# Composed weights stored once in float32 and split after the load, with the end of the count stage reordered

## The chip, the cores and the metric

The kernel runs on one core of a Trainium2 chip. The metric is device time in microseconds (us), the median of several executions. The engines are TensorE (PE, with its weight loads as PEld), VectorE (DVE), ScalarE (ACT), GpSimd (POOL) and SyncE (SP), which here only issues transfers. Two queues of transfers matter: the one that SyncE fills (q1) and the one that GpSimd fills (q0). All of them are served by the same 16 DMA engines.

## The reference

There are 625 nodes with 512 features and 10000 edges, each with 128 attributes and a type, 0 or 1.

```python
m = relu(concat([h[src], edge_attr]) @ W1.T + b1) @ W2.T + b2
agg = segment_sum(m, dst)
# gates r, z, n of a GRU cell from agg and h, batch norm, residual sum
x = layernorm(x + h + bn)
# then two relational layers (relu between them), each:
w = einsum('rb,bio->rio', att, basis)      # 30 bases of 512x512, 2 relations
msg = where(edge_type == 0, sigmoid(x_j @ gate_w[0]) * x_j @ w[0],
                            sigmoid(x_j @ gate_w[1]) * x_j @ w[1])
out = segment_sum(msg, row) + x @ root + bias
```

and at the end `layernorm(x + out)`. The 30 bases of each layer are 31 MB, so reading `basis` for both layers is most of the traffic.

## The kernel before, in words

Most matrix products are done with each operand split into a high part, rounded to the matmul's input format (fp32r), and a low part, the difference; three products of such parts make one full one. ScalarE writes the high part (a copy with a cast) and VectorE the low part (a subtraction).

The program has these stages.

1. **Count** (to 68 us). For 20 windows of 32 nodes VectorE makes one-hot rows (lines 869 and 874), TensorE counts with them (line 1228), ScalarE copies the counts out (lines 635 and 637). In between TensorE composes the first three weight tiles (line 1203), and multiplies x by a part of W1. After window 19 VectorE works out which windows each unit of edges touches (lines 917 to 928, ten small operations on one partition, the result is `wins`), adds the first three attribute rows (line 939), and drains the third early tile (`drain_early`, line 880). Only then, at line 1316, does TensorE clear its banks and start the units: it waits for `ct_drained` of the last window, `early_drained` of all three early tiles, and `wins_ready`.
2. **Units** (68 to 194 us). 20 units of four groups of 128 edges. GpSimd gathers rows, TensorE multiplies attributes (line 1238) and sums messages (lines 1284, 1285), VectorE adds and splits, ScalarE applies relu (line 667).
3. **Jobs** (194 to 512 us). A list, `plan_jobs`, fixes the order of 86 jobs; all engines walk it. Each job fills one of eight PSUM banks, and the job eight places later reuses the bank. A letter in the list says who drains it, "A" for ScalarE and "V" for VectorE. Kinds are RT, agg, r, hn, in, z (the GRU cell), xT (transposes), w (a composed tile), M (a tile of x times a composed weight) and out.

A composed weight does not come out of TensorE in the layout in which M needs it. So each of 16 tiles (`w`, 8 in each layer, 3 of them early) goes to device memory and comes back. Drain of a tile: ScalarE casts the bank into `ev[:, 0]` (line 729, for early tiles line 658), VectorE subtracts it from the bank into `ev[:, 1]` (line 1080, for early tiles line 880), and SyncE stores both halves, 512 KB (line 547; early tiles are stored from ScalarE's queue, line 661). ScalarE may overwrite `ev` only when the store before has landed.

The weights come back by `load_w` on GpSimd's queue (line 594): for each layer and relation 8 loads of 128 KB for the high part and 8 for the low part, 32 in a layer. `w_lo` takes the place of other operands, and so does `w_hi`; in layer 0 the low part of relation 1 is loaded once the last `hn` job is done and the rest once the last `in` job is done. In layer 1 all loads follow the last M job of layer 0 and the last store.

SyncE issues its transfers in the order of the program. The bases of one tile are two transfers of 2 MB each (line 443) into two slots. A slot is refilled when the half tile before it has been composed. In SyncE's order the two basis loads of the next tile come ahead of the store of the current one.

In the z jobs ScalarE takes the sigmoid (line 709), opens the gate of the tile before (line 694) and takes the root of the variance (line 683), each between table loads. VectorE updates the node rows in the same jobs (lines 1031 to 1041).

The high and low rows of the second bias, `b2`, are made in windows 14 and 16 of the count stage (lines 652, 654, 906) and used by the agg jobs.

## Time and profile before

| What | Before |
|---|---|
| median of 3 executions | 513.55 us (511.71 to 514.07) |
| the profiled execution: its own time | 514.26 us |
| its span | 512.4 us |
| TensorE busy | 484.8 us (95%) |
| VectorE busy | 294.4 us (57%) |
| ScalarE busy | 187.3 us (37%) |
| GpSimd busy | 117.3 us (23%) |
| mean granted TensorE clock | 0.989 of full speed |
| bytes moved by DMA | 129.59 MB, 253 GB/s on average |
| stores of composed tiles | 16 of 512 KB |
| loads of composed weights | 64 of 128 KB |

The profile is of one execution, whose own time is 0.7 us above the median. All durations below come from it. Rows of the trace name an engine, a line of the program, and output and input by the names of the tensors; where two tensors share memory, a row can carry the other one's name (`xT_lo` for the place of the second and third early tile, `X` for the work area of the count and unit stages, `RT` for zeros).

### The profile page before, as it was taken

The page shows a single profiled execution, that of the slowest core. Times are in us where ns is not written, and L with a number is a line of the kernel's source. Part 1 is how long each engine was busy: PE and PEld are TensorE (multiplying, and loading weights), DVE is VectorE, ACT ScalarE, POOL GpSimd, SP SyncE. Part 2 cuts the span into 40 slices and gives each one's busy share as a digit, 9 for nine tenths or more (in the row PEclk, how much of TensorE's full clock was granted, in tenths as well). Part 3 has the DMA queues.
Part 4 walks back from the last instruction along what each step waited for, and adds up shares of the span by engine and source line. Part 5 has one row for each costly group of instructions (what it writes and reads, how often), then busy time and mean ns, then how long its engine had stood idle before and what let it go on. Part 6 is the DMA issues. An engine that isn't in the chain of part 4 may idle for free.

```text
span 512.4 us, 6700 instructions
## 1 busy us (share of the span) xinstructions
PE 484.8 (95%) x2230; PEld 299.5 (58%) x2231; DVE 294.4 (57%) x580; ACT 187.3 (37%) x343; POOL 117.3 (23%) x147
## 2 busy tenths in 40 slices
PE   7999969999999998999999999997898999999995
PEld 2444334545454556865575576563664677787774
DVE  5976889898989897382022698545233113341323
ACT  1897943333435334452161214443231011242000
POOL 0000747676667600000000344000000093000000
PEclk9999989999999999999999999998899999999999
DMA  8979987787778729889798799969988484200011
GB/s 255 434 269 346 350 326 225 234 265 259 243 241 267 231 94 393 324 316 379 267 381 336 248 360 349 363 252 400 376 336 322 157 217 114 82 1 1 20 42 42
DMA packets 32790, 129.59 MB, mean 253 GB/s; under 512 B 4794, under 2 KB 7818, under 8 KB 28270
## 3 DMA queue, kind: packets, MB, share of 16 engines
q1 hardware_dynamic: 17518, 95.74, 49.4%
q0 software_dynamic: 11440, 29.11, 19.7%
q10 hardware_dynamic: 3792, 4.22, 2.5%
q8 instruction: 24, 0.39, 0.3%
q14 instruction: 16, 0.13, 0.1%
HBM read 118.04 MB, written 11.01 MB: 252 GB/s over the span
## 4 chain that ended last, share of the span: by engine, by line
PE 76%; DMA 15%; DVE 5%; issue 2%; DVEq 1%; ACT 1%; SPq 0%
PE ps L1343 14%; DMA basis<-in_basis 13%; PE ps L1238 13%; PE ps L1403 10%; PE ps L1442 9%; PE ps L1203 9%; PE ps L1284 5%; PE ps L1285 4%; PE ps L1382 3%; PE ps L1181 3%; PE ps L1170 2%; PE ps L1228 2%; DMA X<-in_eaT 1%; PE ps L1417 1%; DVE x L939 1%
## 5 line engine op out<-in xcount | busy, mean ns | idle before, releaser
L1238 PE MATMUL ps<-X 128*128 128x512 f32 x158 | 73.7, 607 | 0.2 <-DMA X<-in_eaT 0.2
L667 ACT ACTIVATE rhi<-x 128x512 fp32r<-128x512 f32 x79 | 47.1, 631 | 73.1 <-DVE x L939 70.9
L1203 PE MATMUL ps<-basis,sel 128*32 128x512 f32 x496 | 59.8, 612 | 6.6 <-DMA basis<-in_basis 6.6
L585 POOL DMA_INDIRECT X<-u_rows,esrc x40 | 42.4, 1059 | 76.3 <-DMA u_rows<-X 50.8
L946 DVE SCALAR_TENSOR_TENSOR rlo<-x,rhi 128x512 fp32r<-128x512 f32 x79 | 50.7, 684 | 0.2 <-ACT rhi L667 0.2
L1442 PE MATMUL ps<-Xr,CT_r 128*128 128x512 f32 x200 | 47.0, 389 | 0.0
L1238 PEld LDWEIGHTS ps<-X 128*128 128x128 f32 x158 | 29.0, 194 | 28.4 <-issue 28.2
L585 POOL DMA_INDIRECT x_sb<-u_rows,esrc x39 | 41.2, 1056 | 18.8 <-DVE x L939 12.7
L594 POOL DMA_DIRECT2D Xr<-w_layer x32 | 17.7, 832 | 108.0 <-DMA w_layer<-ev 108.0
L1442 PEld LDWEIGHTS ps<-Xr,CT_r 128*128 128x128 f32 x200 | 37.5, 188 | 7.8
L594 POOL DMA_DIRECT2D w_hi<-w_layer x32 | 17.0, 690 | 106.4 <-DMA w_layer<-ev 96.5
L1203 PEld LDWEIGHTS ps<-basis,sel 128*32 128x32 f32 x496 | 14.4, 111 | 39.5 <-issue 27.7
L1284 PE MATMUL ps<-rhi,oh 128*128 128x512 f32 x79 | 33.0, 418 | 2.7 <-DVE rlo L946 0.2
L635 ACT COPY CT<-ps 32x320 f32<-32x320 f32 x80 | 33.3, 417 | 3.7 <-PE ps L1255 2.6
L1075 DVE SCALAR_TENSOR_TENSOR Xr<-ps,gate,Xr 128x512 fp32r<-128x512 f32 x20 | 14.9, 749 | 33.0 <-ACT Xr L744 33.0
L1080 DVE TENSOR_TENSOR ev<-ps,ev 128x512 fp32r<-128x512 f32 x13 | 9.0, 690 | 41.4 <-ACT ev L729 41.2
L1285 PE MATMUL ps<-rlo,oh 128*128 128x512 f32 x79 | 31.0, 392 | 0.0
L939 DVE TENSOR_TENSOR x<-ps,X 128x512 f32<-128x512 f32 x40 | 25.7, 684 | 8.5 <-PE ps L1238 8.5
L1403 PE MATMUL ps<-Xr,xT_hi 128*128 128x512 f32 x120 | 30.3, 395 | 0.0
L1284 PEld LDWEIGHTS ps<-rhi,oh 128*128 128x128 f32 x79 | 14.8, 187 | 21.7 <-issue 19.2
L939 DVE TENSOR_TENSOR x<-ps,x_sb 128x512 f32<-128x512 f32 x39 | 25.0, 684 | 4.1 <-PE ps L1238 4.1
L744 ACT ACTIVATE Xr<-ps,gate 128x512 fp32r<-128x512 f32 x20 | 13.7, 688 | 36.3 <-PE ps L1343 36.3
(213 smaller groups left out, 774.7 us busy)
## 6 DMA issues: line engine op xcount, KB each, us to landing
basis<-in_basis SPq DMA_DIRECT2D x29, 2048.0 KB, 10.4
w_layer<-ev SPq DMA_DIRECT2D x13, 512.0 KB, 11.6
X<-in_eaT SPq DMA_DIRECT2D x20, 256.0 KB, 3.7
basis<-in_basis SPq DMA_DIRECT2D x8, 512.0 KB, 4.4
Xr<-w_layer POOLq DMA_DIRECT2D x32, 128.0 KB, 3.5
w_hi<-w_layer POOLq DMA_DIRECT2D x32, 128.0 KB, 3.5
X<-in_WhhT SPq DMA_DIRECT2D x3, 1024.0 KB, 13.5
basis_apart<-in_basis SPq DMA_DIRECT2D x1, 2048.0 KB, 19.7
```

What stands on the lines that cost most here:

```text
L585: nc.gpsimd.indirect_dma_start(gat[e % GATHERS], None, t["u"][:, :], bass.IndirectOffsetOnAxis(ap=esrc[:, e:e + 1], axis=0)).then_inc(gat_ ...
L594: nc.gpsimd.dma_start(into[64 * c:64 * c + 64, r, k], src[r, k, c, part]).then_inc(done, 16)
L667: nc.scalar.activation(rhi[:, u % 2, s], pre[:, s], ACT.Relu).then_inc(hi_ready, 1)
L939: dve.tensor_tensor(pre[:, s], ps[:, EA_BANKS[s]], gat[e % GATHERS], ALU.add).then_inc(pre_ready, 1)
L946: nc.vector.scalar_tensor_tensor(out=rlo[:, u % 2, s], in0=pre[:, s], scalar=0.0, in1=rhi[:, u % 2, s].bitcast(F32), op0=ALU.max, op1=ALU. ...
L1203: mm = pe.matmul(bank[32 * g:32 * g + 32], sel[:, layer, s], held[:, g, s2], start=(s == 0), stop=(s == 3), tile_position=(0, 32 * g))
L1238: pe.matmul(ps[:, EA_BANKS[s]], eaT[:, u % 2, s * P:(s + 1) * P], W1bT, start=True, stop=True).then_inc(ea_done, 1)
L1284: pe.matmul(into, ones[:, s], rhi[:, u % 2, s], start=False, stop=True, skip_group_check=True)
L1285: mm = pe.matmul(into, ones[:, s], rlo[:, u % 2, s], start=False, stop=True, skip_group_check=True)
L1343: mm = pe.matmul(bank, a[:, k, m * P:(m + 1) * P], w[:, k], start=(start and i == 0), stop=(stop and i == len(terms) - 1))
L1403: mm = pe.matmul(bank, a[k][:, m * P:(m + 1) * P], w[:, k], start=False, stop=(i == parts[-1] and j == len(terms) - 1))
L1442: mm = pe.matmul(bank, counts[:, n, r * NP + m * P:r * NP + (m + 1) * P], half[n][:, r].bitcast(dt), start=False, stop=last)
```

## The change

**Weights.** A tile is drained by ScalarE alone, in float32 (a plain copy), into one of two buffers `ev[:, 0]` and `ev[:, 1]` in turn, and stored as 256 KB. All w jobs have letter "A". The store waits for ScalarE's copy only, and ScalarE waits for the store two tiles before. GpSimd loads 8 transfers of 128 KB for each layer and relation, 16 in a layer, into `w_raw`, the same memory as `w_lo`. The new `split_w` makes the high part on ScalarE (128x2048) and the low part on VectorE (128x2048, in place). In layer 0 it is called after jobs z1 and z3, in layer 1 after out2 and out3. In layer 0 all loads are issued once the last `hn` job is done and all stores have landed. M waits for `w_ready` instead of the loads.

**Count stage.** Early tiles need no VectorE; ScalarE drains each one window after it is composed and stores it in the next window, and the third one goes to `R`. The ten operations for `wins` move from behind window 19 to window 3. The two operations for `b2` on ScalarE move to units 3 and 4, the one on VectorE behind the last unit. Ahead of the unit stage VectorE waits for the last counts before it writes `fold`.

```diff
...
+W_SPLIT_AT = {("z", 1): (0, 1), ("z", 3): (0, 0), ("out", 0, 2): (1, 1), ("out", 0, 3): (1, 0)}
...
-            jobs.append((composed.pop(0), "V"))
+            jobs.append((composed.pop(0), "A"))
...
-        split = [name for name, _ in self.list if name[0] in ("w", "RT", "agg", "xT", "M")]
-        self.upper = {name: n + 1 + EARLY for n, name in enumerate(split)}
+        split = [name for name, _ in self.list if name[0] in ("RT", "agg", "xT", "M")]
+        self.upper = {name: n + 1 for n, name in enumerate(split)}
...
-        ev = sb("ev", [P, 2, H], F32R)
+        ev = sb("ev", [P, 2, H])
...
-        w_lo = Xr[:, 8192:12288].rearrange("p (r k n) -> p r k n", r=REL, k=KT)
+        w_lo, w_raw = (at[:, 8192:12288].rearrange("p (r k n) -> p r k n", r=REL, k=KT) for at in (Xr, X))
...
-        early_ev = [ev, xT_lo[:].rearrange("p k n -> p (k n)")[:, 0:2 * H].rearrange("p (q n) -> p q n", q=2),
-                    xT_lo[:].rearrange("p k n -> p (k n)")[:, 2 * H:4 * H].rearrange("p (q n) -> p q n", q=2)]
+        early_ev = [ev[:, 0], ev[:, 1], R[:, 0:H]]
...
-        w_hi_in = sem("w_hi_in")
-        w_lo_in = [sem("w_lo_in0"), sem("w_lo_in1")]
-        w_out = sem("w_out")
+        w_in = [sem("w_in0"), sem("w_in1")]
+        w_hi_ready = sem("w_hi_ready")
+        w_ready = sem("w_ready")
+        w_out = [sem("w_out0"), sem("w_out1")]
...
-                    sp.dma_start(t["w"][layer][tile], ev[:].bitcast(F32)).then_inc(w_out, 16)
+                    sp.dma_start(t["w"][layer][tile][:, 0], ev[:, tile % 2]).then_inc(w_out[tile % 2], 16)
...
-            def load_w(layer, r, part, into, done):
+            def load_w(layer, r):
...
-                        nc.gpsimd.dma_start(into[64 * c:64 * c + 64, r, k], src[r, k, c, part]).then_inc(done, 16)
-
-
-            pool.wait_ge(w_out, 16 * WT)
-            full(pool, ("hn", NT - 1))
-            load_w(0, 1, 1, w_lo, w_lo_in[1])
-            full(pool, ("in", NT - 1))
-            for r in (1, 0):
-                load_w(0, r, 0, w_hi, w_hi_in)
-            load_w(0, 0, 1, w_lo, w_lo_in[0])
-
-            pool.wait_ge(w_out, 2 * 16 * WT)
-            full(pool, ("M", 0, NT - 1, 0))
-            for r in (1, 0):
-                load_w(1, r, 0, w_hi, w_hi_in)
-                load_w(1, r, 1, w_lo, w_lo_in[r])
+                        nc.gpsimd.dma_start(w_raw[64 * c:64 * c + 64, r, k], src[r, k, c, 0]).then_inc(w_in[r], 16)
+
+            for layer in range(2):
+                for q in range(2):
+                    pool.wait_ge(w_out[q], 16 * (layer + 1) * WT // 2)
+                full(pool, (("hn", NT - 1), ("M", 0, NT - 1, 0))[layer])
+                for r in (1, 0):
+                    load_w(layer, r)
 
         @block.scalar
...
-                if w == 14:
-                    act.wait_ge(rows_in, 16)
-                    nc.scalar.copy(b2, rows).then_inc(b2_parts, 1)
-                    act.wait_ge(b2_parts, 1)
-                    nc.scalar.activation(rows, rows, ACT.Copy, scale=halves[0:36, 0:1]).then_inc(b2_parts, 1)
                 for i in range(EARLY):
                     if w == EARLY_AT[i] + 1:
                         act.wait_ge(early_full, i + 1)
-                        nc.scalar.copy(early_ev[i][:, 0], ps[:, 3 + i % 2]).then_inc(upper_ready, 1)
-                    if w == min(EARLY_AT[i] + 4, WINS - 1):
+                        nc.scalar.copy(early_ev[i], ps[:, 3 + i % 2]).then_inc(early_drained, 1)
+                    if w == EARLY_AT[i] + 2:
                         act.wait_ge(early_drained, i + 1)
-                        act.dma_start(t["w"][0][i], early_ev[i][:].bitcast(F32)).then_inc(w_out, 16)
+                        act.dma_start(t["w"][0][i][:, 0], early_ev[i]).then_inc(w_out[i % 2], 16)
             for u in range(UNITS):
 
                 act.wait_ge(sums_done, u + 1)
...
+                if u == 3:
+                    act.wait_ge(rows_in, 16)
+                    nc.scalar.copy(b2, rows).then_inc(b2_parts, 1)
+                if u == 4:
+                    act.wait_ge(b2_parts, 1)
+                    nc.scalar.activation(rows, rows, ACT.Copy, scale=halves[0:36, 0:1]).then_inc(b2_parts, 1)
...
-            act.wait_ge(w_out, 16 * EARLY)
+            act.wait_ge(w_out[0], 16 * 2)
...
+            def split_w(layer, r):
+
+                act.wait_ge(w_in[r], 16 * 2 * KT * (layer + 1))
+                nc.scalar.copy(w_hi[:, r], w_raw[:, r]).then_inc(w_hi_ready, 1)
...
-                    if kind == "r":
+                    if kind == "w":
+
+                        act.wait_ge(w_out[nw % 2], 16 * (nw // 2))
+                        ins = nc.scalar.copy(ev[:, nw % 2], bank)
+                        nw += 1
+                    elif kind == "r":
                         ins = nc.scalar.activation(x1[:, name[1]], bank, ACT.Sigmoid)
...
-                    if kind == "w":
-
-                        act.wait_ge(w_out, 16 * nw)
-                        nw += 1
-                        ins = nc.scalar.copy(ev[:, 0], bank)
-                    elif kind == "RT":
+                    if kind == "RT":
...
+                if name in W_SPLIT_AT:
+                    split_w(*W_SPLIT_AT[name])
...
-            def drain_early(i):
-
-                dve.wait_ge(upper_ready, i + 1)
-                dve.tensor_tensor(early_ev[i][:, 1], ps[:, 3 + i % 2], early_ev[i][:, 0].bitcast(F32), ALU.subtract
-                                  ).then_inc(early_drained, 1)
-
...
-                if w == 16:
-                    dve.wait_ge(b2_parts, 2)
-                    nc.vector.scalar_tensor_tensor(out=b2, in0=b2.bitcast(F32), scalar=halves[0:36, 1:2],
-                                                   in1=rows, op0=ALU.mult, op1=ALU.add).then_inc(b2_ready, 1)
+                if w == 3:
+
+                    by_unit = sprow[:, 0:2].rearrange("p q (u s) -> p q u s", s=UNIT)
+                    dve.tensor_reduce(uspan[:, 0], by_unit[:, 0], AX.X, ALU.min)
+                    step(dve.tensor_reduce(uspan[:, 1], by_unit[:, 1], AX.X, ALU.max))
...
-                for i in range(EARLY):
-                    if w == EARLY_AT[i] + 4:
-                        drain_early(i)
-
...
-            dve.wait_ge(wins_ready, 1)
...
-            drain_early(EARLY - 1)
+            dve.wait_ge(ct_acc, WINS)
...
+            dve.wait_ge(wins_ready, 1)
...
+            dve.wait_ge(b2_parts, 2)
+            nc.vector.scalar_tensor_tensor(out=b2, in0=b2.bitcast(F32), scalar=halves[0:36, 1:2],
+                                           in1=rows, op0=ALU.mult, op1=ALU.add).then_inc(b2_ready, 1)
+            dve.wait_ge(b2_ready, 1)
...
+            def split_w(layer, r):
+
+                dve.wait_ge(w_hi_ready, 2 * layer + (2, 1)[r])
+                dve.tensor_tensor(w_lo[:, r], w_raw[:, r], w_hi[:, r].bitcast(F32), ALU.subtract).then_inc(w_ready, 1)
...
-                    elif kind == "w":
-                        dve.wait_ge(upper_ready, jobs.upper[name])
-                        ins = dve.tensor_tensor(ev[:, 1], bank, ev[:, 0].bitcast(F32), ALU.subtract)
...
+                if name in W_SPLIT_AT:
+                    split_w(*W_SPLIT_AT[name])
...
-                        pe.wait_ge(w_hi_in, 32 * REL * KT * (layer + 1))
-                        pe.wait_ge(w_lo_in[r], 32 * KT * (layer + 1))
+                        pe.wait_ge(w_ready, 2 * layer + (2, 1)[r])
...
```

What it does to VectorE's order behind window 19 of the count stage. Before (`uspan`, `winf`, `winp` and `wins` are the ten small operations, `xT_lo` the third early tile, `X<-ident` is `fold`):

```order
L917 TENSOR_REDUCE uspan<-sprow 1x20
L918 TENSOR_REDUCE uspan<-sprow 1x20
...
L927 TENSOR_SCALAR winp<-winp 1x20
L928 TENSOR_TENSOR wins<-winp,uspan 1x20
L939 TENSOR_TENSOR x<-ps,X 128x512 x3
L880 TENSOR_TENSOR xT_lo<-ps,xT_lo 128x512
L979 TENSOR_REDUCE X<-ident 128x32
L955 TENSOR_TENSOR oh<-iota,dstf 128x512
L946 SCALAR_TENSOR_TENSOR rlo<-x,rhi 128x512
```

Of the changed kernel, the same place:

```order
L927 TENSOR_TENSOR x<-ps,X 128x512 x3
L967 TENSOR_REDUCE X<-ident 128x32
L449 TENSOR_LOAD wins
L943 TENSOR_TENSOR oh<-iota,dstf 128x512
L934 SCALAR_TENSOR_TENSOR rlo<-x,rhi 128x512
```

The ten operations and the subtraction of the third early tile are gone from behind the windows.

ScalarE's order in the z jobs 1 and 2. Before (`W2T<-ps` is the sigmoid, `sd` the root, `gate` the gate of the tile before):

```order
L709 ACTIVATE W2T<-ps 128x512
L694 ACTIVATE gate<-gate 128x2
L683 ACT_TABLE_LOAD
L683 ACTIVATE sd<-mv,epst 128x1
L709 ACT_TABLE_LOAD
L709 ACTIVATE W2T<-ps 128x512
```

Of the changed kernel:

```order
L713 ACTIVATE W2T<-ps 128x512
L694 CAST w_hi<-X 128x2048
L688 ACTIVATE gate<-gate 128x2
L677 ACT_TABLE_LOAD
L677 ACTIVATE sd<-mv,epst 128x1
L713 ACT_TABLE_LOAD
L713 ACTIVATE W2T<-ps 128x512
```

The high part of a composed weight is cast between the sigmoid and the root; VectorE's row `Xr<-X,w_hi 128x2048` stands behind its update of the same tile.

## Rows read from the trace of the kernel before

**Rows 1.** The page, busy time and its share of the span, instructions of each engine

```profile
PE 484.8 (95%) x2230; PEld 299.5 (58%) x2231; DVE 294.4 (57%) x580; ACT 187.3 (37%) x343; POOL 117.3 (23%) x147
```

**Rows 2.** Waits of TensorE: what it waited for, us in total, times, longest

```profile
PE ps L1203 <- DMA basis<-in_basis: 6.6, 5, 3.2
PE ps L1316 <- DVE xT_lo L880: 4.1, 1, 4.1
```

**Rows 3.** Timeline, end of the count stage: start, us, engine, work [idle before]

```profile
63.70 0.22 DVE L917 TENSOR_REDUCE uspan<-sprow 1x20 f32<-1x80 f32 x1
...
64.53 1.70 ACT L635 COPY CT<-ps 32x320 f32<-32x320 f32 x4 [0.20 <-PE ps L1255]
...
65.39 0.17 DVE L928 TENSOR_TENSOR wins<-winp,uspan 1x20 int32<-1x20 f32 x1
...
66.23 0.16 ACT L637 COPY X<-ps 128x1 f32<-128x1 f32 x1
...
67.40 0.68 DVE L880 TENSOR_TENSOR xT_lo<-ps,xT_lo 128x512 fp32r<-128x512 f32 x1
```

**Rows 4.** Timeline, first matmul behind the count stage, a clearing of a bank

```profile
68.56 1.06 PE L1316 MATMUL ps<-RT 128*128 128x512 bf16 x2 [4.07 <-DVE xT_lo L880]
```

**Rows 5.** Windows: stretch, us, PE, PEld, DVE, ACT, POOL busy, PEclk, DMA share, GB/s

```profile
68.00:70.00 2.00, 1.44 (x4) 0.74 (x6) 1.65 (x4) 1.46 (x3) 1.70 (x2) 0.50 1.02 424
70.00:72.00 2.00, 2.00 (x5) 1.03 (x4) 0.10 (x1) 0.21 (x1) 0.01 (x1) 0.65 1.01 412
...
358.00:360.00 2.00, 2.00 (x10) 0.62 (x3) 0.00 (x0) 0.57 (x1) 0.00 (x0) 0.50 0.96 401
...
388.00:390.00 2.00, 0.50 (x8) 0.20 (x12) 0.00 (x0) 0.00 (x0) 0.00 (x0) 1.00 0.65 152
```

**Rows 6.** Timeline, early in the count stage, the one-hots and counts of window 4

```profile
23.24 1.14 DVE L874 TENSOR_SCALAR X<-iota,keyf 128x320 bf16<-128x320 f16 x5
...
25.21 0.57 PE L1228 MATMUL ps<-X 128*128 128x321 bf16 x3
```

**Rows 7.** Groups of instructions by line: count, busy us, mean ns, idle before

```profile
L667 ACT ACTIVATE rhi<-x 128x512 fp32r<-128x512 f32 x79 | 47.1, 631 | 73.1 <-DVE x L939 70.9 <-DVE xT_lo L880 2.2
...
L1080 DVE TENSOR_TENSOR ev<-ps,ev 128x512 fp32r<-128x512 f32 x13 | 9.0, 690 | 41.4 <-ACT ev L729 41.2 <-DVE W2T L1041 0.2
...
L1118 DVE TENSOR_TENSOR root_lo<-W2T,xT_low 128x2048 fp32r<-128x2048 f32 x2 | 4.6, 2292 | 2.0 <-ACT xT_low L784 2.0
L784 ACT CAST xT_low<-W2T 128x2048 fp32r<-128x2048 f32 x2 | 3.8, 1900 | 0.0
...
L906 DVE SCALAR_TENSOR_TENSOR bn_r<-bn_r,halves,bn 36x512 fp32r<-36x512 f32 x1 | 0.7, 745 | 0.8 <-ACT bn L654 0.8
```

**Rows 8.** Timeline, the second halves of three composed tiles that TensorE waited for

```profile
325.87 1.93 PE L1203 MATMUL ps<-basis,sel 128*32 128x512 f32 x16 [1.26 <-DMA basis<-in_basis]
...
355.72 3.64 PE L1203 MATMUL ps<-basis,sel 128*32 128x512 f32 x16 [3.25 <-DMA basis<-in_basis]
...
389.50 1.92 PE L1203 MATMUL ps<-basis,sel 128*32 128x512 f32 x16 [1.58 <-DMA basis<-in_basis]
```

**Rows 9.** DMA queues from 311 to 325 us: packets, MB, share

```profile
q1 hardware_dynamic: 353, 4.30, 87.6%
q0 software_dynamic: 330, 0.55, 13.0%
```

**Rows 10.** Timeline: update in z3, low part of xT for tile 1, product that reads it

```profile
335.15 0.69 DVE L1031 TENSOR_TENSOR x<-W2T,x 128x512 f32<-128x512 f32 x1 [5.29 <-ACT W2T L709]
...
340.31 0.69 DVE L1084 TENSOR_TENSOR xT_lo<-ps,xT_hi 128x512 fp32r<-128x512 f32 x1 [0.21 <-DVE W2T L1041]
...
347.74 1.07 PE L1343 MATMUL ps<-w_hi,xT_hi 128*128 128x512 f32 x4
```

**Rows 11.** Timeline, layer 1: the last loads of weights and the first product

```profile
422.41 4.56 POOL L594 DMA_DIRECT2D Xr<-w_layer  x8
...
440.09 1.17 PE L1343 MATMUL ps<-w_hi,xT_hi 128*128 128x512 f32 x4
```

23 lines of the change are left out of this document (10 added, 13 removed).

## The prediction

> **What bounds the kernel now.** I read the page first: TensorE is busy for 484.8 of 512.4 us, 95% [rows 1]. No other engine is above 57%. So what an edit frees on VectorE, ScalarE or the DMA engines is worth nothing by itself; only TensorE's idle time, 27.6 us in all, and its clock can be won. Second, the waits of TensorE: 6.6 us in five waits for basis loads, and one wait of 4.1 us ahead of the unit stage [rows 2]. The second is a wait for the very subtraction (line 880) that the change removes; the first depends on how busy the DMA engines are, and the change removes traffic. Third, the timeline of these places shows who is late [rows 3, 4, 6, 8]. Fourth, the windows show the granted clock behind each idle stretch [rows 5]. A change of 0.5%, 2.6 us, is about what a measurement of this kernel tells from none.
>
> **End of the count stage.** Behind the last one-hots VectorE runs the ten operations for `wins`, from 63.70 to 65.56, three additions, and the subtraction of the third early tile from 67.40 to 68.08. TensorE starts at 68.56, 0.48 us behind it [rows 3, 4]. In the changed kernel TensorE needs three things there. `wins` is ready since window 3. The third early tile is drained by ScalarE's copy between windows 17 and 18. What is late next is ScalarE's copying of window 19, which ends at 66.39 (66.23 plus 0.16) [rows 3]. With the same 0.48 us behind it TensorE starts at 66.87, 1.7 us earlier. ScalarE had waited 0.20 us for the count of window 19, which now comes sooner, since VectorE no longer has one subtraction and the `b2` operation (0.7 us plus a wait of 0.8 [rows 7]) in windows 15 and 16. I take 0.1 of that: **1.8 us**. Bounds: 0 if gathered rows or the loads of attributes are late instead, and 2.2 if all of the count stage's end moves up. VectorE's new wait for the last counts ends before ScalarE's copy of them does, so it adds nothing; the additions ahead of it end near 65.7.
>
> **TensorE's clock there.** TensorE had been idle for 4.07 us when it started [rows 4]. Its clock was granted at 0.50 from 68 to 70 and 0.65 from 70 to 72 [rows 5]: it had fallen to 1.2 GHz, and came back to 2.4 GHz about 1.4 us into the second window. TensorE was busy at half clock for 1.44 us and then 1.4, 2.84 in all, of which full clock would have saved half, 1.4 us. Behind an idle stretch of 3.25 us it had also fallen: 16 matmuls took 3.64 us, elsewhere 1.92 [rows 8], and the window at 358 shows 0.50 [rows 5]. Behind 1.58 us it had not: the window at 388 shows 1.00 [rows 5, 8]. The new idle stretch is 4.07 less 1.8, 2.3 us, between these. It is nearer to the 1.58 that did no harm than to 3.25, so I take the larger part of the 1.4: **1.3 us**; bounds 0 and 1.4. The Trainium skill ("TensorE: Matmul & The Clock Gate", What's actually happening) says that half clock is the default which activity releases, and that the point of change differs from run to run of one kernel. By that rule the length of the idle stretch alone doesn't settle the term: the sum would be 509.3 in some executions and 510.6 in others. One profiled execution can't show this.
>
> **The ten operations in window 3.** They took 1.86 us behind window 19 [rows 3] and take it now ahead of the one-hots of window 4. Those ran from 23.24 to 24.38, and TensorE counted with them from 25.21, in steps of 0.17 us against VectorE's 0.23 [rows 6]. Pushed by 1.86 they run from 25.10 to 26.24: the first is ready at 25.33, and the fifth count ends about 0.3 us later than before. Behind window 6 VectorE waits for TensorE in each window, so the rest is absorbed. I take **minus 0.3 us**; bounds 0 and minus 1.9.
>
> **b2 moved.** On ScalarE its two operations now stand in units 3 and 4, where ScalarE waits 70.9 us in all for VectorE's additions, 3.5 us in each of 20 units [rows 7]: nothing. On VectorE the operation of 0.75 us now stands behind the last unit, where VectorE has no idle time before TensorE's transposes need it; in the same chain the subtraction for the first composed tile of the jobs, 0.69 us, goes [rows 7]. **Minus 0.1 us.**
>
> **Draining a tile.** 13 subtractions of 690 ns leave VectorE, 9.0 us [rows 7]. None is a thing that TensorE waited for in [rows 2], and the cover is TensorE's own work, so nothing is won directly; the store of a tile is issued 0.7 us earlier. SyncE issues the next two basis loads ahead of that store, so nothing is queued behind its wait that TensorE needs at once.
>
> **Traffic.** 16 stores go from 512 to 256 KB and 64 loads of 128 KB become 32: 4 + 4 MB of 129.6. What matters is which of the five basis waits shared the DMA engines with it. Behind 325.87 TensorE waited 1.26 us [rows 8]. From 311 to 325 us, while that load of 2 MB and its pair went through q1 (4.30 MB), q0 still carried 0.55 MB of composed weights [rows 9]. In the changed kernel GpSimd issues 16 loads, not 32, from about 287 us on, which are done near 307. Then the 0.55 MB is gone; at the 4.85 MB in 14 us of [rows 9] it is worth 1.6 us, more than the wait: **1.3 us**. At 355.72 (3.25 us) and 389.50 (1.58 us) [rows 8] no weight loads were under way, and the store stands behind the basis loads in its queue. 3.25 stays, of the 1.58 and the two short waits (0.5 us together) the halved stores may take a little: **0.3 us**, bounds 0 and 2.1. The Trainium skill ("DMA: Bandwidth & Descriptors", Bandwidth) speaks against the halved stores: it wants transfers of at least 1 MiB for three quarters of peak, so 256 KB would gain less than half of what 512 KB cost. By it the 0.3 would be nearly 0 and the sum 509.6. The count of loads is halved at the same size, so the 1.3 isn't touched by it.
>
> **The splits.** Each is a ScalarE cast of 1.90 us and a VectorE subtraction of 2.29 us on 128x2048 [rows 7], four pairs, 16.8 us of work. Layer 0: ScalarE does them right behind the sigmoids of z1 and z3, ahead of the gate and the root of the same job, so VectorE's update is held up by at most 1.90 us and what follows it then by its own 2.29. The tightest reader is the product of M for tile 1: it started at 347.74 and the low half of xT that it reads was written from 340.31 to 340.99, 6.75 us before [rows 10]. The split at z3 pushes that write by at most 4.2 us; what z1 pushed, as much, is absorbed ahead of z3, where VectorE waits 5.29 us for the sigmoid [rows 10]. 2.5 us of cover are left: **0**. Layer 1: the last of 32 loads was issued at about 427, and the first product started at 440.09 [rows 11]. Eight loads take 4.56 us to issue, so 16 of them are issued some 9 us sooner, and both splits stand in jobs out2 and out3, the later of which ends some 8 us ahead of that product; a pair takes 4.2 us: **0**.
>
> **Sum.** 1.8 + 1.3 - 0.3 - 0.1 + 1.3 + 0.3 = 4.3 us. The profiled execution took 514.26, so it would take 510.0. It lies 0.7 above the median of 513.55, so the median is forecast at **509.3 us**. The unit stage behind the first two terms keeps TensorE busy nearly without a gap, so they should be carried through to the end.
>
> **Rivals.**
> Clock falls all the same behind the 2.3 us: 509.3 + 1.3 = 510.6. For it: 3.25 us sufficed. Chance 0.15.
> Basis waits stay, since the loads are held by something else than the weights: 509.3 + 1.6 = 510.9. For it: four of the five waits had no weight loads beside them. Chance 0.12.
> The clock doesn't fall behind the 3.25 us, because the waits around it shift: 509.3 - 1.7 (3.64 less 1.92 [rows 8]) = 507.6. Against it: nothing shortens that wait. Chance 0.08.
> The reordering doesn't do what it says: VectorE bounds the early windows, so its 1.9 us in window 3 is all paid, and the end of the stage only gives it back: 509.3 + 1.6 = 510.9. For it: between windows 2 and 6 VectorE has almost no idle time. Chance 0.08.
> Slower: the two splits of layer 0 lie on the path between z1 and the product at 347.74. Their price is 2 x (1.90 + 2.29) = 8.4 us, so 517.7. It decides from the point where a weight load lands later than its split wants it (317 and 335 us): ScalarE then stands at `w_in` with the next sigmoid, tile drain and xT queued behind it, VectorE behind that, and the cover of 2.5 us is gone. For it: q0 got only 0.55 MB in 14 us beside the basis loads [rows 9]. Against it: the loads start 14 us earlier and there are half as many. Chance 0.05.
> The forecast itself has 0.52.
>
> **How the numbers follow.** The predicted time is the forecast's. Range: low is 509.3 less the 1.7 of the second clock fall and 1.2 of the other waits, 506.4; high takes two rivals of 1.3 and 1.1 together, 511.7. Above lie the slower rival and the worst pairs, below next to nothing; under 2 in 10. Faster by over 0.5% means under 511.0: the forecast nearly always, the third rival, and about two thirds of the three that end near 510.6 to 510.9, which noise splits: 0.77. Slower by over 0.5%: 0.05. Same: 0.18.
>
> **What would show it.** Right: the clearing of banks starts near 66.9 with under 2.5 us of idle before it, the clock stays at 1.00 from 66 to 74, TensorE waits for basis loads about 5 us in all with none near 324, and the M products wait for no split. Wrong: a new wait of ScalarE's cast for a load, of the M product for VectorE's `Xr` row, of the counts of windows 4 or 5 for one-hots, or a window at 0.50 near 68.

## The result and the profile after

| What | Before | After |
|---|---|---|
| median | 514.38 us (511.71 to 518.72, 22 executions) | 511.95 us (509.56 to 514.39, 22 executions) |
| ratio after / before | | 0.9949 (95% interval 0.9930 to 0.9968) |
| profiled execution | 514.26 us, span 512.4 | 510.66 us, span 508.9 |
| TensorE busy | 484.8 us | 483.9 us |
| mean granted TensorE clock | 0.989 | 0.991 |
| bytes moved by DMA | 129.59 MB | 121.20 MB |

The changed kernel is faster by 0.5%, 2.4 to 2.6 us. 4.3 us were forecast, and 511.95 lies above the upper end of the range, 511.7. The sign was right and the size was not. Of the 2.65 us between 509.3 and 511.95, 0.8 are the kernel before itself: the forecast started from 513.55, the median of 3 executions, and 22 executions have 514.38. The other 1.9 us are missing gain.

A few executions of some runs, in a slower state of the chip, are in the medians and ranges below and not in the ratios.

The page of the changed kernel, to be held against [rows 1]:

```profile
PE 483.9 (95%) x2231; PEld 299.2 (59%) x2231; DVE 293.1 (58%) x568; ACT 194.3 (38%) x347; POOL 100.3 (20%) x115
```

Waits of TensorE (line, what it waited for, us in total, times, longest), against [rows 2]:

```profile
PE ps L1313 <- ACT X L630: 3.6, 1, 3.6
PE ps L1200 <- DMA basis<-in_basis: 3.2, 2, 2.6
...
PE ps L1200 <- issue: 1.4, 3, 0.7
...
PE ps L1225 <- DVE X L875: 1.1, 2, 0.8
```

Basis waits fell from 6.6 us to 3.2. The wait ahead of the unit stage is for ScalarE now, as forecast, but 3.6 us long, not 2.3. Waits for one-hots are 1.1 us in two, where before one of 0.7 stood ahead of window 19; 0.83 of it is at a new place, window 4. 1.4 us of "issue" (time for which the profile has no releaser) in the middle of a composed tile are new.

VectorE and TensorE in windows 3 and 4, timeline of the changed kernel (start, us, engine, work, idle before), against [rows 6]:

```profile
22.65 0.22 DVE L902 TENSOR_REDUCE uspan<-sprow 1x20 f32<-1x80 f32 x1
...
24.35 0.17 DVE L913 TENSOR_TENSOR wins<-winp,uspan 1x20 int32<-1x20 f32 x1
25.17 0.83 DVE L870 SCALAR_TENSOR_TENSOR X<-X 128x640 bf16<-128x640 f16 x1 [0.65 <-issue]
25.91 1.15 DVE L875 TENSOR_SCALAR X<-iota,keyf 128x320 bf16<-128x320 f16 x5
```

```profile
26.35 1.07 PE L1225 MATMUL ps<-X 128*128 128x321 bf16 x5 [0.83 <-DVE X L875]
...
29.95 1.09 PE L1225 MATMUL ps<-X 128*128 128x321 bf16 x6
```

The ten operations take 1.87 us, 22.65 to 24.52, and VectorE then stands for 0.65 us before it starts the codes of window 4, with no releaser in the trace. The one-hots start at 25.91 instead of 23.24, TensorE's counts at 26.35 instead of 25.21, and the counts of window 5 at 29.95 against 28.25 before. The delay is not absorbed; it grows to 1.7 us, and to 2.0 at window 6 (32.91 against 30.91).

The end of the count stage, same view, ScalarE and then TensorE, against [rows 3, 4]:

```profile
60.00 0.16 ACT L630 COPY X<-ps 128x1 f32<-128x1 f32 x1
63.39 1.71 ACT L628 COPY CT<-ps 32x320 f32<-32x320 f32 x4 [3.23 <-remote]
...
69.57 1.70 ACT L628 COPY CT<-ps 32x320 f32<-32x320 f32 x4
71.28 0.16 ACT L630 COPY X<-ps 128x1 f32<-128x1 f32 x1
```

```profile
61.13 0.18 PE L1252 MATMUL ps<-RT 128*128 128x32 bf16 x1
62.05 1.06 PE L1200 MATMUL ps<-basis,sel 128*32 128x512 f32 x8 [0.74 <-issue]
63.35 1.02 PE L1200 MATMUL ps<-basis,sel 128*32 128x512 f32 x2 [0.24 <-issue]
64.77 1.12 PE L1200 MATMUL ps<-basis,sel 128*32 128x512 f32 x6 [0.40 <-issue]
...
71.49 2.32 PE L1313 MATMUL ps<-RT 128*128 128x512 bf16 x5 [3.60 <-ACT X L630]
```

From 60.2 to 63.4 ScalarE does nothing, though the counts of window 17 are complete at 61.31. "remote" means that the profile has no releaser for it. VectorE stands from 59.65 to 62.16, which the profile puts down to counts of TensorE that were done at 61.31, and again 1.2 us before 65.30; TensorE crawls through 16 matmuls of a composed tile that elsewhere take 1.92 us, from 62.05 to 65.89. All three stop in the same stretch. I call this the **standstill**. The clearing begins at 71.49, 2.9 us later than before, where 66.9 was forecast.

Windows from 68 to 76 and at 358 us (columns as in [rows 5]):

```profile
68.00:70.00 2.00, 0.00 (x0) 0.00 (x0) 1.86 (x4) 1.92 (x7) 1.63 (x2) 0.85 0.62 161
70.00:72.00 2.00, 0.51 (x2) 0.23 (x3) 0.00 (x0) 1.97 (x6) 1.63 (x2) 0.50 1.02 354
...
74.00:76.00 2.00, 2.00 (x3) 0.67 (x2) 0.45 (x1) 0.00 (x0) 0.00 (x0) 0.50 0.95 380
...
358.00:360.00 2.00, 2.00 (x14) 1.11 (x7) 0.00 (x0) 0.59 (x1) 0.00 (x0) 1.00 1.11 475
```

The clock is at 1.2 GHz from 70 to 76 this time: TensorE works some 4.7 us at it behind the clearing, where before it was 2.8. It didn't fall behind the basis wait of 2.64 us at 356.82, where it fell before behind 3.25 us.

Between fixed points of TensorE's program (first clearing, first transpose of the sums, first product of r, first transpose for xT, first product of M, first output product, end), span of after less span of before: +2.9 up to the clearing, +0.7 in the unit stage, +0.2 up to r, -2.2 up to xT, 0.0 up to M, -5.2 up to the outputs, 0.0 from there. The sum is -3.5, the difference of the spans. So the count stage and the unit stage lost 3.6 us where 2.8 were to be won, and the later stages won 7.2 where 1.5 were forecast. The two misses have opposite signs, and the total is near the forecast only since they cancel.

### The profile page after: what moved, and what is told of

The parts are those of the page before. It is cut to its first block, busy times and chain, and to the rows that moved or that the text cites. A ratio compares the mean times of both kernels' runs of the same rounds, so it can differ in the third digit from the quotient of the medians.

```text
span 508.9 us, 6645 instructions
## 1 busy us (share of the span) xinstructions
PE 483.9 (95%) x2231; PEld 299.2 (59%) x2231; DVE 293.1 (58%) x568; ACT 194.3 (38%) x347; POOL 100.3 (20%) x115
## 2 busy tenths in 40 slices
DMA packets 29206, 121.20 MB, mean 238 GB/s; under 512 B 4282, under 2 KB 7306, under 8 KB 24686
## 4 chain that ended last, share of the span: by engine, by line
PE 83%; DVE 5%; DMA 5%; ACT 2%; issue 2%; DVEq 1%; another core or an unknown queue 1%; SPq 0%
PE ps L1400 17%; PE ps L1340 16%; PE ps L1235 13%; PE ps L1200 9%; PE ps L1438 9%; PE ps L1281 5%; DMA basis<-in_basis 5%; PE ps L1282 4%; PE ps L1379 3%; PE ps L1167 3%; ACT CT L628 2%; PE ps L1225 1%; PE ps L1178 1%; PE ps L1414 1%
## 5 line engine op out<-in xcount | busy, mean ns | idle before, releaser
L1200 PE MATMUL ps<-basis,sel 128*32 128x512 f32 x496 | 58.7, 596 | 4.6 <-DMA basis<-in_basis 3.2
L595 POOL DMA_DIRECT2D X<-w_layer x32 | 16.9, 653 | 214.4 <-DMA w_layer<-ev 214.4
L1400 PEld LDWEIGHTS ps<-Xr,xT_hi 128*128 128x128 f32 x120 | 22.1, 188 | 5.7 <-issue 1.2
L870 DVE SCALAR_TENSOR_TENSOR X<-X 128x640 bf16<-128x640 f16 (+1 forms) x21 | 16.8, 799 | 14.8 <-PE ps L1225 9.4
```

Source lines behind the costliest of these rows:

```text
L1200: mm = pe.matmul(bank[32 * g:32 * g + 32], sel[:, layer, s], held[:, g, s2], start=(s == 0), stop=(s == 3), tile_position=(0, 32 * g))
L1400: mm = pe.matmul(bank, a[k][:, m * P:(m + 1) * P], w[:, k], start=False, stop=(i == parts[-1] and j == len(terms) - 1))
```

## Experiments

All are edits of the changed kernel unless said otherwise. Each group ran on one chip, with its own runs of before; ratios are to those. The third and the fourth group ran on the same chip, the others on two more. The changed kernel ran in each as control.

### First group: the place of the ten operations

**The changed kernel again.** No edit.

> The changed kernel once more, for a second look at the stretch from 60 to 66 us, where in its first profile ScalarE, TensorE and VectorE all stood still for 3.2, 1.4 and 1.2 us with no wait that the profile can name. Theory: (a) the ten operations in window 3 are paid in full, 1.9 us, in every execution, so window 6 is again counted near 32.9 us (before: 31.0); (b) the standstill is instruction fetching behind the gathers, which depends on where the program stands when the DMA engines are full, so it is there again, 3 to 4 us. Clearing again starts near 71.5, time 510.5 to 513. Rival: the standstill was a disturbance of one execution; then clearing starts near 68 and the time is 508 to 510.

507.43 us (506.07 to 511.03), ratio 0.9883 (0.9846 to 0.9919). The profile has no standstill: TensorE waits 0.92 us for the basis at 61.74 and the clearing begins at 68.57. The counts of windows 4 and 6 begin at 26.1 and 32.7, against 25.2 and 30.9 before: the loss in window 3 is there again.

**Operations behind window 19**, as before the change; all else as changed.

```
-                if w == 3:
-
-                    by_unit = sprow[:, 0:2].rearrange("p q (u s) -> p q u s", s=UNIT)
-                    dve.tensor_reduce(uspan[:, 0], by_unit[:, 0], AX.X, ALU.min)
...
                 if w == 2:
...
+            by_unit = sprow[:, 0:2].rearrange("p q (u s) -> p q u s", s=UNIT)
+            dve.tensor_reduce(uspan[:, 0], by_unit[:, 0], AX.X, ALU.min)
...
             def add_rows(u, tiles):
```

> The changed kernel with the ten operations for wins put back behind window 19. Theory: window 3 costs 1.9 us; put back, windows 4 to 6 are counted as early as in the kernel before, and the end doesn't need wins before ScalarE's last copy, so it is 1.5 to 2.5 us faster than the changed kernel, near 509.5. Rival: window 3 is absorbed by the later windows and the loss lies only in the standstill; then it is within 0.5 us of the changed kernel.

506.78 us (505.53 to 509.03), ratio 0.9859 (0.9828 to 0.9890). Counts of windows 4 and 6 at 25.2 and 30.9 as before; clearing at 67.07, 1.5 us earlier than the control. VectorE's operations behind window 19 cost nothing now, since ScalarE sets the end.

**Operations spread**, one in each of the windows 7 to 16.

```
-                if w == 3:
+                if w == 7:
...
+                if w == 8:
                     step(nc.vector.scalar_tensor_tensor(out=uspan[:, 2], in0=uspan[:, 1], scalar=1.0,
...
+                if w == 16:
                     dve.tensor_tensor(wins[:], winp[:, 1], uspan[:, 0], ALU.add).then_inc(wins_ready, 1)
```

> The changed kernel with the ten operations for wins one by one in windows 7 to 16, where VectorE waits 0.6 to 1.2 us for TensorE in each window. Theory: hidden there, so as e2, 1.5 to 2.5 us faster than the changed kernel, and clearing starts 1.9 us earlier in the profile. Rival: any operation of VectorE in the count stage is on the path; then as the changed kernel.

506.0 us (504.05 to 508.36), ratio 0.9860 (0.9826 to 0.9895). TensorE in windows 4 and 5 and at the clearing, timeline of this run:

```profile
25.19 0.85 PE L1232 MATMUL ps<-X 128*128 128x321 bf16 x5
...
28.22 0.99 PE L1232 MATMUL ps<-X 128*128 128x321 bf16 x6
```

The wait for one-hots is gone, the windows are where they were before the change, and the clearing begins at 67.12 behind 3.39 us of idle time. In this execution the clock didn't fall behind it:

```profile
66.00:68.00 2.00, 0.88 (x5) 0.61 (x7) 0.60 (x1) 1.98 (x6) 0.60 (x1) 1.00 1.02 409
68.00:70.00 2.00, 2.00 (x6) 0.94 (x5) 1.05 (x3) 0.64 (x2) 0.00 (x0) 1.00 1.03 425
```

So the ten operations cost 1.5 us in window 3 at the clearing, and 0 behind window 19 or where VectorE has idle time. The medians of the three runs differ by 0.7 and 1.4 us in the same sense, but their intervals overlap; the profiles carry this verdict.

**The reordering of the count stage alone**: the kernel before, its composed weights still stored and loaded in two parts and its early tiles still drained by both engines, with the ten operations in window 3 and b2 moved as changed.

```
+                if w == 3:
+
+                    by_unit = sprow[:, 0:2].rearrange("p q (u s) -> p q u s", s=UNIT)
...
+            dve.wait_ge(ct_acc, WINS)
...
+            dve.wait_ge(wins_ready, 1)
...
+            dve.wait_ge(b2_ready, 1)
```

> The kernel before with the count stage's reordering alone: wins in window 3, b2 in the units, VectorE's wait for the last counts; weights still split ahead of the store, early tiles still drained by VectorE. Theory: it costs 1.9 us in window 3 and wins back at most what wins and the clearing's wait gave, about 1.9 less what ScalarE's copies still hold, so it is 0 to 2 us slower than the kernel before; the basis wait near 326 (1.3 us) and the ones near 355 and 389 stay. Rival: the reordering is a gain by itself, 1 to 2 us faster than before.

515.35 us (511.16 to 521.07), ratio 1.0017 (0.9990 to 1.0045): nothing won. The clearing begins at 69.06, 0.5 us later than before: TensorE's idle time ahead of it is 0.5 us shorter (3.57 for 4.07) and starts 1.0 us later (65.5 for 64.5). The basis waits at 253.64 (0.62), 328.26 (1.93) and 358.50 (3.58) are there. The whole gain of the changed kernel on this chip (0.9883 against 1.0017, 6.9 us) comes from the rest of the change: the weights, with the drain of the early tiles.

### Second group: which traffic

**Control**, no edit.

> The changed kernel once more, as the control for the three runs beside it. In the first session it ran 0.995 of the time of before, in the second 0.988; its first profiled execution stood still for some 3 us in two places between 60 and 66 us (VectorE and TensorE waiting without a releaser in the trace), and the clearing of the banks began at 71.49; in the second session at 68.57. Theory (the changed kernel takes one of two courses there, by execution, and its own time is the second's): 507 to 508, ratio to before 0.987 to 0.990, clearing at 68.5, no standstill. Rival (the standstill belongs to the kernel, whose early gathers of rows fill the DMA engines, and comes in about half of the executions): ratio between 0.988 and 0.996 and an interval over 3 us wide. Both: TensorE starts the counts of window 4 some 1.1 us later than before (26.3 for 25.2).

512.36 us (510.07 to 516.20), ratio 0.9947 (0.9912 to 0.9981). Standstill in the profile (ScalarE 3.2 us), clearing at 71.50.

**Each weight loaded twice**, so the loads are as many as before the change.

```
-                for r in (1, 0):
-                    load_w(layer, r)
+                load_w(layer, 1, w_raw, w_in)
+                if layer == 0:
+                    full(pool, ("in", NT - 1))
+                for r in (1, 0):
+                    load_w(layer, r, w_hi, w_twice)
+                load_w(layer, 0, w_raw, w_in)
```

> The changed kernel, but each composed weight is loaded twice, once more into w_hi ahead of the float32 load, as many loads as before the change (64 of 128 KB in all), in its order and with its gates. Theory (the halved loads took away the wait for the basis at 325.87): the wait of 1.3 us near 324 comes back, and perhaps the small ones at 236 and 252 (0.28 and 0.26), r to xT0 goes from 104.3 back to 105.6 to 106.4, the time up by 1.3 to 2 us over the control: 508.5 to 509.5 where the control has 507.3. Rival (it was the store, or chance): the wait stays away, within 0.5 us of the control.

517.50 us (514.30 to 520.98), ratio 1.0063 (1.0030 to 1.0097): 5.1 us over the control. The wait that the changed kernel had lost is back, in the place of [rows 8]'s first row:

```profile
329.54 1.92 PE L1206 MATMUL ps<-basis,sel 128*32 128x512 f32 x16 [2.49 <-DMA basis<-in_basis]
```

The theory holds in place and not in size: 2.5 us in this profile, 5 in the median. The edit puts the float32 load of relation 0 behind 16 more loads; no product of M waits for it.

**Each tile stored twice**, to both halves of its place: the stores move 8 MB as before.

```
-                    sp.dma_start(t["w"][layer][tile][:, 0], ev[:, tile % 2]).then_inc(w_out[tile % 2], 16)
+                    for half in range(2):
+                        sp.dma_start(t["w"][layer][tile][:, half], ev[:, tile % 2]).then_inc(w_out[tile % 2], 16)
```

> The changed kernel, but each composed tile is stored twice, to both halves of its place, so that the stores move 8 MB as before the change; the loads are as in the changed kernel. Theory (stores cost nothing: they stand behind the basis loads in their queue): within 0.5 us of the control, no wait near 324. Rival (the stores share the DMA engines with the next basis loads and cost as much as the loads of weights do): waits for the basis appear at 236, 252 or 326 and at 390, 1 to 2 us more.

517.01 us (513.63 to 518.50), ratio 1.0040 (1.0010 to 1.0070): 4.7 us over the control. My theory that the stores cost nothing falls. The profile has waits for the basis of 3.39 us at 358.70, 0.84 at 405.39 and 0.40 at 256.18, which the control has not, or shorter; but the control has 1.34 at 388.58, which this one has not, and the sums are near (5.2 and 4.7). The clearing begins at 72.22, 0.7 us later than in the control. So the profile doesn't show where the 4.7 us are.

**Clock kept ahead of the clearing**: the spread variant with 12 matmuls of zeros in the idle time.

```
+            pe.wait_ge(early_drained, 2)
+            for _ in range(12):
+                pe.matmul(ps[:, 4], zer[:, 0:P], zer, start=True, stop=True)
             pe.wait_ge(ct_drained, WINS)
```

> The variant with the ten operations for the window numbers spread one by one over windows 7 to 16, and with 12 extra 128x512 matmuls of zeros into bank 4 as soon as the third early tile is drained, ahead of the wait for the last drains of the count stage. They fill part of the 3.4 us for which TensorE stood idle there; their results are overwritten. Theory (the clock that TensorE had after the idle time fell in four of five profiles and costs 1.4 us or more): granted clock 1.00 from 66 to 74, the clearing at 67.1 to 67.5, and 0.5 to 1.4 us less in the median than the spread variant's 0.986 of before, that is 504.6 to 505.6. Rival (the clock isn't held by work that ends before the last wait, or the extra matmuls end late): clock at 0.50 there all the same, time as the spread variant or up to 1 us more.

509.01 us (506.28 to 509.90), ratio 0.9883 (0.9836 to 0.9931), against the control's 0.9947. The extra matmuls run from 65.61 to 68.36, the clearing follows at 69.30, and the clock holds:

```profile
68.00:70.00 2.00, 1.06 (x6) 0.35 (x5) 0.19 (x1) 1.97 (x6) 1.50 (x2) 1.00 1.03 388
70.00:72.00 2.00, 2.00 (x7) 1.01 (x6) 1.05 (x2) 0.81 (x2) 0.00 (x0) 1.00 0.97 403
```

The clearing is late since this execution has the standstill too (ScalarE idle for 3.9 us before 61.19). Against the spread variant's 0.9860 on another chip nothing can be said of the clock's price; the 3.3 us to the control beside it are the spread operations and the clock together.

### Third group: what stops three engines

**Control**, no edit.

> The changed kernel a fourth time, as the control for the three runs beside it. It has run at 0.995, 0.988 and 0.995 of the time of before on three chips; the two profiles at 0.995 show a standstill of VectorE, ScalarE and TensorE between 60.1 and 63.4 us, the one at 0.988 does not. Theory (the standstill makes the difference between sessions): with the standstill in the profile the ratio is 0.993 to 0.996, without it 0.986 to 0.990. Rival (the sessions differ for another reason): ratio and standstill do not go together.

511.43 us (509.86 to 513.25), ratio 0.9926 (0.9900 to 0.9952); standstill, clearing at 71.36. The ratio is just below what the theory gave for a profile with standstill.

**Gathers 4 to 7 held** until the first addition.

```
-                if e >= GATHERS:
+                if e >= UNIT:
...
-                    pool.wait_ge(pre_ready, 4 + e - GATHERS + 1)
+                    pool.wait_ge(pre_ready, 4 + max(e - GATHERS, 0) + 1)
```

> The changed kernel, but GpSimd issues the gathers of rows 4 to 7, which the second unit reads, only when VectorE has made its first addition of the unit stage (near 63), not from 59 us on. Theory (the three engines stand still at 60 to 63 us because the next instructions are fetched by the DMA engines and queue behind eight gathers of 256 KB): no standstill in the profile even where the control has one, the clearing at 68.0 to 69.0, and 2.5 to 3.5 us less than a control with standstill, or 0 to 0.5 less than one without. Rival 1 (the fetch is slow by itself, whatever the gathers do): standstill stays, time as the control. Rival 2 (the held gathers are late for the second unit): VectorE waits for them behind 72 us and what was won is lost.

The standstill is gone. ScalarE in the same stretch, timeline of this run:

```profile
60.21 1.70 ACT L628 COPY CT<-ps 32x320 f32<-32x320 f32 x4
61.92 0.16 ACT L630 COPY X<-ps 128x1 f32<-128x1 f32 x1
62.10 1.71 ACT L628 COPY CT<-ps 32x320 f32<-32x320 f32 x4
```

The clearing begins at 68.92, and the profiled execution took 507.56 us against the control's 510.64. The DMA queues from 58 to 66 us, first in the changed kernel's first profile and then here, show what changed (packets, MB, share):

```profile
q0 software_dynamic: 628, 2.06, 67.8%
q1 hardware_dynamic: 55, 0.58, 18.1%
...
q8 instruction: 1, 0.02, 0.8%
q14 instruction: 1, 0.01, 0.2%
```

```profile
q1 hardware_dynamic: 519, 1.57, 55.9%
q0 software_dynamic: 314, 1.02, 32.0%
...
q8 instruction: 1, 0.02, 0.8%
q14 instruction: 1, 0.01, 0.2%
```

In both, two packets of instructions move through the same DMA engines in this stretch. With 2.06 MB of gathered rows there, three engines stop; with half of it they don't. That is no rule, though. Queue 0 in the same stretch of the changed kernel in the first group, which has no standstill, and of the run with both kinds of traffic doubled (fourth group), which has one:

```profile
q0 software_dynamic: 466, 1.53, 49.0%
```

```profile
q0 software_dynamic: 343, 1.15, 40.1%
```

All four profiles of the first group issue their eight gathers by 64.2, have both instruction packets, and stand still nowhere. So what is shown is that on this chip the held gathers go with no standstill in three profiles of three, and gathers not held with one in five of five. Neither the gathers nor the packets are enough for it. The median, though, is 511.56 us (507.56 to 511.87), ratio 0.9916 (0.9885 to 0.9947), the same as the control: the 3 us that the profile shows are not in the median, and ratio and standstill do not go together here. Either other executions have another course, or the held gathers cost elsewhere; only one execution per run is profiled, so this is open.

**Spread, clock kept, gathers held**: the three edits together.

> All three edits that have each shown something: the ten operations for the window numbers spread one by one over windows 7 to 16, 12 extra matmuls of zeros in the idle time ahead of the clearing, and gathers 4 to 7 held until the first addition. Theory (the three add up: 1.4 to 1.9 us for the operations, 1.4 for the clock, up to 3 for the standstill): ratio to before 0.980 to 0.984, 504 to 506, granted clock 1.00 at the clearing, counts of window 4 at 25.2. Rival (they overlap: without the standstill TensorE's idle time and its clock are other than with it): 0.985 to 0.988.

508.88 us (506.45 to 509.97), ratio 0.9867 (0.9834 to 0.9900). Counts of window 4 at 25.3, extra matmuls at 63.34, clearing at 66.65 at full clock, no standstill: each place is as meant, 4.7 us earlier than in the control's profile. But two new waits stand in the unit stage at 96 to 98 us (0.56 and 0.81), and the time is 2.6 us under the control. The ratio is in the rival's range (they overlap), 0.985 to 0.988.

**The same with the second clock kept**: 10 extra products between the halves of the tile that waits at 353.

```
+                    if group == 0 and other is not None:
+                        for _ in range(10):
+                            pe.matmul(other, xT_hi[:, 0, 0:P], w_hi[:, 1, 0], start=True, stop=True)
```

> As the run before, and in the wait for the basis near 353 us TensorE runs 10 extra 128x512 float32r matmuls (about 2.3 us) between the two halves of that composed tile, into the next job's bank, which is drained by then and overwritten later. Theory (the clock that falls behind 2.6 to 3.3 us of idle time costs 1.7 us: 3.5 us instead of 1.9 for the 16 matmuls behind it): granted clock 1.00 from 350 to 365, 1 to 1.7 us less than the run before, in those executions in which the clock would have fallen. Rival (the extra work is longer than the wait, or delays the next basis load): time as the run before or up to 1 us more, with the wait gone but the work behind it later.

508.04 us (506.64 to 509.51), ratio 0.9860 (0.9831 to 0.9889). TensorE there, timeline of this run:

```profile
350.82 2.60 PE L1214 MATMUL ps<-w_hi,xT_hi 128*128 128x512 f32 x10
353.77 1.92 PE L1207 MATMUL ps<-basis,sel 128*32 128x512 f32 x16 [0.35 <-DMA basis<-in_basis]
```

The extra work fills the wait, and the clock holds from the count stage to the last microseconds. The gain over the run before, 0.8 us, is smaller than what either median is uncertain by.

### Fourth group: do the prices of traffic add

**Both stored and loaded twice**, 129.6 MB as before; the diffs are those of the two single runs.

> The changed kernel with both kinds of traffic as before the change: each composed tile stored twice and each weight loaded twice, 129.6 MB in all. All else is the changed kernel's. Theory (each half of the traffic shares the DMA engines with the basis loads, and their prices add): against the control beside it 9 to 10 us more, that is a ratio to before of 1.01 to 1.02, with waits for the basis near 252, 312, 329 and 405. Rival 1 (the two prices overlap, since the same basis load can be late only once): 5 to 7 us over the control, ratio 1.003 to 1.008, as the run with the count stage's changes alone (1.0017). Rival 2 (the traffic is worth little, and doubled stores and loads cost something that before did not have): ratio above 1.02.

521.75 us (520.24 to 527.37), ratio 1.0112 (1.0071 to 1.0152), 9.3 us over the control beside it: the prices add. Of the 9.8 us of the two single runs nearly all is here. Waits of TensorE in its profile (527.37 us, the longest of its runs):

```profile
PE ps L1208 <- DMA basis<-in_basis: 10.2, 5, 4.9
PE ps L1321 <- ACT X L636: 7.0, 1, 7.0
```

The same bytes cost more here than in the kernel before (1.0112), and more than in the run with the reordering alone (1.0017, on another chip). This run has two stores of 256 KB for one of 512 KB; whether that is the reason is not shown. Queue 10 of this profile has 4224 packets for 4.22 MB, that of before 3792. The row of this run:

```profile
q10 hardware_dynamic: 4224, 4.22, 2.5%
```

**Loads twice, another execution**, one only.

> The run with each weight loaded twice, for one more profiled execution: its first profile was the fastest of its 12 executions (514.3 against a median of 517.5) and showed one new wait of 2.5 us for the basis near 329. Theory (in most executions more of the basis loads are late): an execution near 517 shows two or more further waits for the basis between 236 and 312 or near 390, 2 to 3 us together. Rival (the rest of the 5 us is no wait but the clock): the same wait alone and one more stretch at granted clock 0.5.

516.98 us, basis waits of 8.1 us in four: 0.97 at 51.44, 3.11 at 330.69, 2.57 at 359.92, 1.50 at 392.31. Against the control's profile of this group (3.4 us in two) that is 4.7 us more, the size of the median's difference. Of the waits expected between 236 and 312 none came, and 1.3 to 1.6 us near 390 stand in the profiles of before and of one control too. The first profile had caught a short execution.

**Stores twice, another execution**, one only.

> The run with each tile stored twice, for one more profiled execution (the first: 515.66 against a median of 517.01, with waits for the basis of 0.4 at 256, 3.4 at 359, 0.8 at 405 and the attributes 0.5 at 54). Theory (stores hold up basis loads in places that change from one execution to the next): waits for the basis of 6 to 8 us in all, at other places. Rival: the same four waits, and what is left of the 4.7 us is in the clock.

516.43 us, with basis waits of 4.9 us only (4.7 and 3.4 in the two controls), so the theory falls. What is new is at the end of the count stage, where ScalarE stands still at three places. Waits of ScalarE from 40 to 80 us:

```profile
ACT R L647 <- remote: 4.0, 1, 4.0
ACT CT L629 <- remote: 3.6, 2, 2.6
```

TensorE's idle time ahead of the clearing is 9.10 us, and the clearing begins at 75.57. It is 4.4 us later than in the control beside it. The stores of the early tiles fall into the stretch of the gathers (0.52 MB in queue 10 from 58 to 66 us, for 0.23), and the standstill grows; that the one makes the other is a guess. In this execution most of the price of the doubled stores is here and not in the waits for the basis.

**Control**, no edit.

> The changed kernel beside these three, as their control and for a fifth profile of it. Theory: ratio to before between 0.988 and 0.995; waits for the basis 4 to 5 us in all; if VectorE and ScalarE stand still at 60 to 63 us, the clearing begins near 71.4, else at 68.6.

512.42 us (510.43 to 514.30), ratio 0.9943 (0.9920 to 0.9967). Standstill (0.88 and 0.40 us of "issue" within the tile at 61.87), clearing at 71.19. Basis waits 3.4 us.

## Why the prediction was wrong

Up to the clearing, the profiles give a ladder: 67.07 and 67.12 us with the ten operations elsewhere, 68.57 with them in window 3, 71.49 with the standstill on top, and behind that more time at the low clock. The forecast had 66.9, or 67.1 with its own price of window 3.

**The ten operations in window 3** (minus 0.3 us) is the first step that failed; it measured minus 1.5. The step took VectorE's 1.86 us off a start of TensorE at 25.21 that had slack for the first one-hot only, and then had the rest absorbed by the waits behind window 6. In the runs the delay was 0.9 to 1.1 us at window 4 and 1.7 to 2.2 at window 6, in all profiles with the operations in window 3 and in none without them, and 1.5 at the clearing where nothing else came between. Two things were missed. VectorE's idle time behind window 6 is time in which it waits for TensorE, and TensorE, which bounds the stage, has little to give back: of 1.8 us at window 6 in the first group's control, 1.5 reached the clearing. And the price on VectorE was 1.87 + 0.65 us, the second part a stop at "issue". The fourth rival named this mechanism and gave it 0.08.

**End of the count stage** (1.8 us) was nearly right by itself: in the spread run the clearing begins at 67.12, 1.4 us earlier than before, with ScalarE's last copies setting it as forecast. In the changed kernel window 3 took all of it, and a standstill came on top, for which the sum had no term: 2.9 us between 68.57 and 71.49, the largest piece of the miss. It is in all ten profiles without held gathers of the first session and the second to fourth groups, in none of the four of the first group. Its cause stays open.

**The clock there** (1.3 us) was not won. The step subtracted the 1.8 us from TensorE's idle time, but TensorE's counts end earlier too (its idle time began at 63.7 in the spread run, 64.5 before), and the idle time was 3.2 to 3.6 us, not 2.3. After such an idle time the clock fell in 11 of 12 profiles. In the first profile the term has the other sign: 4.7 us of work at the low clock for 2.8, which by half of the difference costs 1.0 us more than before and fits the 0.7 us that the unit stage lost. The Trainium skill ("TensorE: Matmul & The Clock Gate", What's actually happening) says of the point at which the clock is released that it differs from run to run of one kernel. Here the fall differs too: at the wait of 2.6 to 3.6 us near 355 the clock fell in 10 of the 17 profiles, that of before among them, that had it, with 2.57 us in one and not with 3.27 us in another. A single profile of before that shows a fall and a single one of after that shows none can differ by chance. In before TensorE worked at the low clock from 355.7 to 361.5; half of these 5.8 us, 2.9, is in the 5.2 us won between M and the outputs in the first pair. The rest is the two basis waits there, 3.25 and 1.58 us before and 2.64 after.

**The splits** (0) were right: between the first transpose for xT and the first product of M lie 17.2 us in before and in the changed kernel, and no product waits for a split in any run. **b2** cost 0.2 us between the transposes and r, where 0.1 was forecast.

**Traffic** (1.3 + 0.3 us) was right in its place and too small. The wait at 325.87 went, in the first profile the two short ones ahead of it too; the loads doubled bring it back at 2.5 to 3.1 us. But doubling the loads or the stores back costs about 5 us each in the median. The step that took 0.3 for the stores argued from their place in SyncE's queue, and that place doesn't make them free. That they hold up other transfers through the DMA engines, which all queues share, fits the later clearings of the doubled runs (72.22 and 75.57), but no run separates it. The Trainium skill ("DMA: Bandwidth & Descriptors", Bandwidth) asks for transfers of at least 1 MiB; by an estimate from that rule the halved stores would have brought nearly nothing. The run with doubled stores doesn't test it, since it sends 256 KB twice and not 512 once; its 4.7 us say only that 16 more stores are not free.

**The range and the chances** do not follow from the rivals as written. The upper end takes two rivals of 1.3 and 1.1 us; the rivals are priced at 1.3, 1.6 and 1.6, and 1.3 with 1.6 gives 512.2, above the 511.95 that was measured. The terms listed for "faster" add to about 0.82, not 0.77.

So the gain of 2.4 us is a large one in the later stages, given back in the first 75 us. The reordering alone (1.0017) and the moved ten operations (clearing 1.5 us earlier) show it but for the standstill. The other four sessions had ratios of 0.9883, 0.9947, 0.9926 and 0.9943, gains of 2.6 to 6.2 us, and the forecast's 4.3 us lies among them; a forecast of this size can't be told right or wrong by one session. Why the ratio was 0.9883 in the first group and 0.9926 to 0.9949 in the four other sessions stays open. The standstill goes with it, but holding the gathers removed it from three profiles and did not move the median.

The best versions measured are the spread run (0.9860), and the one with all edits (0.9860), 506.0 and 508.0 us on their chips. Both beat the kernel before by 1.4%; the second is 3.4 us under its control, the first 1.4 under its own, within what these medians tell.

## What to carry to other kernels

A move of small operations to an early place is free only if the engine that bounds the stage has slack there; look for the idle time of the bound, not of the engine that gets the work. Spread over windows in which their own engine waits, the same ten operations cost nothing. And traffic that no engine waits for can still cost several microseconds beside loads that the bound does wait for. Doubling it tells whether it is free; as a price it was too high here, 9.3 us for both kinds, where the change without its reordering won 6.9.

## What was not expected of the hardware

Three compute engines stopped in one stretch for about 3 us when eight gathers of 256 KB had been issued and the DMA engines carried instruction packets; with four gathers held back it was gone in three profiles of three. But in the first group's four profiles it was absent with all eight gathers and both packets. With twice the stores ScalarE's stop was 4.7 us in one execution, and 2.6 and then 4.0 in another. That the engines waited for instructions fits "remote" and "issue" as releasers. It also fits the packet records of the traces: in seven of the ten profiles with a standstill ScalarE's first copy behind the stop starts 0.2 to 0.4 us behind the end of the 8 KB packet of queue 14 (63.39 behind 63.16 in the first). In the other three it doesn't (61.19 against 61.52, 61.99 against 63.02, 66.02 against 63.16), and the packets themselves took 0.31 us with and without a standstill. So it was only argued.

Of the clock: behind an idle time of 7.0 and 9.1 us TensorE worked at 1.2 GHz for 4.5 and 4.7 us, no longer than behind 3.6 us in the changed kernel's first profile (4.7). 12 matmuls of zeros in the idle time kept it at 2.4 GHz in three profiles of three; without them, behind idle times of 3.2 to 3.6 us, it stayed there in 1 of 12.
